# A four-layer graph network on one core: TensorE's turns and ScalarE's copies of them put at other places of the second and third layer, and the load of x first in SyncE's queue in the third

## Chip, cores and metric

One core of one Trainium2 chip runs the whole program. The time is the device time of one execution in microseconds (us). Engines are named as in the profile: PE is TensorE (PEld its weight loads), DVE is VectorE, ACT is ScalarE, POOL is GpSimd, SP is SyncE, which here only issues DMA transfers.

## What is computed

There are 50000 nodes with 128 features (x) and 12500 edges (src, dst), sorted by dst. Four layers follow one another, each of the form x = layernorm(x + layer(x)):

- layer 0: attention over the edges of a node, four heads, softmax by segment;
- layer 1 (the *second* layer): the mean of the neighbours' rows, then relu(([h, mean] @ W1 + b1) @ W2 + b2);
- layer 2 (the *third* layer): the sum over the edges of h[src] @ Wr[relation], eight relations;
- layer 3: messages by edge type, then one of three weight sets by node type, on [relu(h), sums].

```python
x = _layernorm(x + _L1_gnn_ref(x, src, dst, W1, b1, W2, b2))
x = _layernorm(x + _L2_gnn_ref(x, weight, src, dst, edge_type_8))
```

Only nodes that are the dst of some edge (targets) get anything from the sums. All other nodes go through the four layers on their own (the *dense* path), so nodes and edges are worked on at the same time.

## The kernel before

**Tiles.** A block or chunk is C = 500 rows, kept as R = 125 partitions by T = 4 rows. There are NC = 100 dense blocks of nodes and EC = 25 chunks of edges in each layer. For products a tile is *turned* (transposed by TensorE in four pieces into PSUM, `turn`, L1130) and copied by ScalarE into SBUF with features on 128 partitions.

**The dense path.** Block d passes three steps that lie LAG = 3 blocks apart: load and bias (xin, y0), normalize to x1, turn and copy to xt, product with wab (z); then y1, normalize to x3, turn and copy with relu to rt, the type products (three weight sets at once, into po beside z) and the selection sel, normalize to res, store to out. In one dense step the kernel therefore turns x3 of block d-LAG (`turn_rt`, L1175) and x1 of block d (`turn_xt`, L1182). Both use the PSUM bank pt, so the second turn waits until ScalarE has copied the first. `dense_products` (L1195) waits until DVE has read po of the step before (s_read), writes the bias, adds the type products (L1148) and z (L1207) and raises s_z, on which DVE's `read` waits.

**The second layer** (`for c in range(EC)`, L1319 on PE, L818 on DVE, L1054 on ACT, L327 on SP, L522 on POOL) handles edge chunk c with dense block 52 + c. The source rows xs come by a load by SP (L304) and then, where a source is itself a target, four indirect gathers by POOL over it (L434). The target rows xd, same and aux come by three loads of SP (`targets1`, L306) on the semaphore aux. xs has three buffers, xd, same and aux two. `rows1(c+2)` and `targets1(c+1)` wait for s_ln of chunk c-1, that is until DVE has written the scales nmr (L671) of that chunk, after which its rows are not read any more. PE turns xs and xd through one bank pc, one after the other (`turns1`, L1293), and ACT copies them to st and dt (L973, L978). `products1` (L1302) forms the products of both; the product with agg (L1322) ends the chunk. DVE scans st into run and agg (`source_sums1`, L791), adds, measures and writes the scales.

An iteration of ACT: copy rt and xt of the dense step, copy st and dt of chunk c+1, the roots of chunk c (Ln, Exp on the variances, L921), wait for s_ln, then six groups of four normalizing activations (L918): x3, x1, so, so3, do, res. SP stores so and so3 when nS is raised (behind so3), do when nD is, res when s_out is (L314 to L336). SP's queue is in order: load of x, load of xs, three loads of targets1, stores of so, so3, do, res.

**The third layer** (L1351 on PE, L852 on DVE, L1077 on ACT, L372 on SP, L546 on POOL) handles chunk c with dense block 79 + c. DVE multiplies st with (rel == r) into masked for eight relations (L838), the first EARLY = 2 of them one iteration ahead, between the variances and the scales; PE adds the eight products up in pb (`relations2`, L1337, 16 matmul records a chunk); DVE scans pb into run; PE turns that back to rows in pa (L1356). Its iteration before: pa, turn of x3, turn of x1, all relations of c+1, turn of xs of c+2 (`turns2`, L1331), dense products. ACT's: copy rt and xt, copy st of chunk c+2, roots, x3, x1, do, res. SP's: `sources2(c+3)` (waits until xs of chunk c+1 has been turned), load of x, rel, xd and same, stores of do and res. POOL's: four gathers of xs, bias on x (L449, waits for xin), four gathers of node types.

Of the kernel before, what the change touches and what calls it, by code (L numbers as in the profile page):

```python
# [13 lines left out]
D = 128  # L14
R = 125
T = 4
# [29 lines left out]
def gnn_kernel(nc, x, src, dst, srcP, dstP, nextP, eattrT, etype3, etype8, eweight, ntype3, ntypeP, Wq, Wk, Wv, We, gate,  # L46
# [26 lines left out]
    with ctx:  # L73
# [122 lines left out]
        def _(sp):  # L196
# [175 lines left out]
            for c in range(EC):  # L372
                d = block_of(2, c)
                if there(c + 3):
                    sources2(c + 3)
                if d + 2 < NC:
                    load_dense(d + 2)
                if there(c + 2):
                    relations2(c + 2)
                if there(c + 1):  # L380
                    targets2(c + 1)
                if c >= 1:
                    store2(c - 1)
                store_dense(d - 7)
# [526 lines left out]
        def _(act):  # L911
# [16 lines left out]

            def rows_of(d, s, groups):

                first, second = groups
                if 0 <= d - LAG < NC:
                    normalize(x3[(d - LAG) % 4], y1[(d - LAG) % 4], s, second).then_inc(s_x3, 1)
                if 0 <= d < NC:
                    normalize(x1[d % 4], y0[d % 4], s, first).then_inc(s_x1, 1)
# [191 lines left out]
        def _(pe):  # L1127
# [66 lines left out]

            def dense_products(d):  # L1195

                first, second = (0 <= d - k < NC for k in (0, LAG))
                if first or second:
                    pe.wait_ge(s_read, d + 3)
                    biased_slots(NT + 1)  # L1200
                if second:
                    pe.wait_ge(s_rt, d - 2)
                    last = types(lambda j: rt[:, j, :], 0)
                if first:
                    pe.wait_ge(s_xt, d + 1)
                    for j in range(T):
                        last = mm(po[0:R, j * 512 + NT * D:(j + 1) * 512], xt[:, j, :], wab[:, 0, :], start=False, stop=True, skip_group_check=True)  # L1207
                if first or second:
                    last.then_inc(s_z, 1)
# [83 lines left out]
            def turns1(c):  # L1293
                b, q = c % 2, ph[1]
                pe.wait_ge(q["g"][b], counted(c, 16 * T))
                pe.wait_ge(q["aux"][b], counted(c, 48))
                pe.wait_ge(q["eD"], c)
                turn(pc, xs[c % 3]).then_inc(q["tS"], 1)
                pe.wait_ge(q["eS"], c + 1)
                turn(pc, xd[b]).then_inc(q["tD"], 1)  # L1300

            def products1(c):  # L1302
# [4 lines left out]
                product(pa, lambda j: tile_of(st, j), wab[:, 0, :])  # L1307
                pe.wait_ge(q["eD"], c + 1)
# [8 lines left out]
            turns1(0)  # L1317
            products1(0)
            for c in range(EC):  # L1319
# [17 lines left out]
            def relations2(c):  # L1337
                q = ph[2]
                pe.wait_ge(q["vA"], c)
                for r in range(REL):  # L1340
# [8 lines left out]
            relations2(0)  # L1349
            turns2(1)  # L1350
            for c in range(EC):  # L1351
# [88 lines left out]
```

## Time and profile before

| | us |
|---|---|
| runs, median (lowest to highest) | 2155.61 (2153.47 to 2155.76) |
| profiled execution, its own time | 2157.94 |
| its span, first to last instruction | 2155.8 |
| PE busy | 1613.2 (75%) |
| DVE busy | 1479.8 (69%) |
| POOL busy | 1385.2 (64%) |
| ACT busy | 1087.1 (50%) |
| mean granted TensorE clock | 0.85 |

The span is the time between the first and the last instruction of the profiled execution; the execution's own time is 2.1 us more. Busy shares are means over four layers of different kinds. In the windows the granted clock is 1.00 at 2.4 GHz and 0.50 at 1.2 GHz, and the DMA share is the mean busy share of the core's 16 DMA engines. A word such as "issue" in the chain is time in which an engine waited for nothing that the profile can name.

### The profile page before, as it was taken

How to read it: one execution, taken by the hardware profiler on the slowest of the kernel's cores; microseconds unless marked ns; L12 is line 12 of the kernel's file. 1: busy time of each engine (PE TensorE's matmuls, PEld its weight loads, DVE VectorE, ACT ScalarE, POOL GpSimd, SP SyncE). 2: the span in 40 equal slices, each digit the busy share in tenths (PEclk: the TensorE clock that was granted, in tenths of full speed). 3: DMA queues.
4: the chain of work that ended last, by engine and by line, in shares of the span. 5: the costliest groups of instructions: out<-in, count | busy, mean ns of one | idle time of the engine just before them, and what ended most of it. 6: DMA issues, size and time to landing. Idle time of an engine off the chain costs nothing.

```text
span 2155.8 us, 23908 instructions
## 1 busy us (share of the span) xinstructions
PE 1613.2 (75%) x6303; PEld 993.3 (46%) x6303; DVE 1479.8 (69%) x4219; ACT 1087.1 (50%) x2688; POOL 1385.2 (64%) x1060
## 2 busy tenths in 40 slices
PE   3777777777776377776776677777778499999995
PEld 1444444444444255555554344444444145555553
DVE  4788999988889377677776667776677444444453
ACT  0466666666666466777667243444343323233322
POOL 6888877788884667776660656555664146656663
PEclk7688888888888687888778788888889699999998
DMA  4333333333331344444443333333232122222221
GB/s 122 83 84 91 92 90 92 94 91 90 95 91 53 94 120 142 148 141 141 140 139 98 100 93 89 99 99 95 86 94 73 53 58 72 63 60 64 71 60 27
DMA packets 150726, 198.86 MB, mean 92 GB/s; under 512 B 54874, under 2 KB 82844, under 8 KB 150592
## 3 DMA queue, kind: packets, MB, share of 16 engines
q1 hardware_dynamic: 92992, 173.20, 25.7%
q0 software_dynamic: 57600, 24.15, 6.6%
q8 instruction: 51, 0.84, 0.2%
q14 instruction: 83, 0.68, 0.1%
HBM read 140.85 MB, written 70.88 MB: 98 GB/s over the span
## 4 chain that ended last, share of the span: by engine, by line
PE 58%; ACT 17%; issue 12%; DVE 7%; POOL 3%; DMA 2%; SPq 1%; POOLq 0%; ACTq 0%; DVEq 0%
PE po L1148 19%; PE pb L1342 10%; PE pt L1133 7%; ACT x L918 6%; PE po L1143 4%; ACT res L918 3%; PE pc L1133 3%; ACT st L973 3%; PE po L1207 2%; PE pb L1154 2%; DVE masked L838 2%; ACT do L918 1%; PE pc L1238 1%; ACT so L918 1%; PE pb L1379 1%
## 5 line engine op out<-in xcount | busy, mean ns | idle before, releaser
L434 POOL DMA_INDIRECT xs<-target_rows,slot_all x300 | 405.7, 1352 | 246.7 <-DMA xs<-source_rows 97.1
L918 ACT ACTIVATE x<-y,nmr,rst 125x128 f32<-125x128 f32 x800 | 318.5, 481 | 80.1 <-DVE nmr L671 80.0
L1148 PE MATMUL po<-wnt,rt 128*125 128x384 f32 x800 | 310.9, 537 | 0.2 <-ACT rt L948 0.2
L1133 PE MATMUL pt<-ident,x 125*128 125x125 f32 x800 | 144.2, 310 | 199.0 <-issue 182.4
L449 POOL TENSOR_TENSOR y<-xin,bias_bc 125x512 f32<-125x512 f32 x100 | 133.7, 1338 | 205.9 <-DMA xin<-in_x 201.4
L1148 PEld LDWEIGHTS po<-wnt,rt 128*125 128x125 f32 x800 | 174.2, 218 | 117.8 <-issue 40.8
L1342 PE MATMUL pb<-masked,wr 128*128 128x500 f32 x400 | 218.1, 709 | 1.5 <-DVE masked L838 1.5
L441 POOL DMA_INDIRECT out_rows<-do,last_all x100 | 120.2, 1202 | 145.2 <-ACT do L918 107.9
L838 DVE SCALAR_TENSOR_TENSOR masked<-rel,st 128x500 f32<-128x500 int32 x200 | 121.6, 670 | 132.8 <-ACT st L973 132.8
L1133 PEld LDWEIGHTS pt<-ident,x 125*128 125x128 f32 x800 | 105.2, 162 | 232.5 <-issue 207.0
L1143 PE MATMUL po<-ball,ones_bf 128*125 128x512 bf16 (+1 forms) x512 | 163.4, 452 | 51.1 <-DVE sel L688 48.7
L1148 PE MATMUL po<-wnt,run 128*125 128x384 f32 x600 | 197.6, 486 | 0.0
L918 ACT ACTIVATE do<-yd,nmr,rst 125x128 f32<-125x128 f32 x400 | 163.8, 480 | 56.0 <-DVE nmr L671 56.0
L643 DVE BATCH_NORM_STATS2 bst<-y 125x6 f32<-125x128 f32 x800 | 164.8, 279 | 3.6
L973 ACT ACTIVATE st<-pc 128x500 f32<-128x500 f32 x50 | 29.4, 587 | 272.1 <-PE pc L1133 272.1
L717 DVE TENSOR_TENSOR_SCAN run<-same,run,masked 128x500 f32<-128x500 f32 x75 | 89.3, 1243 | 111.6 <-DMA same<-same_d 85.9
L434 POOL DMA_INDIRECT xs<-in_x,src_all x100 | 130.9, 1309 | 50.3 <-issue 27.8
L918 ACT ACTIVATE res<-sel,nmr,rst 125x128 f32<-125x128 f32 x400 | 161.4, 480 | 1.7 <-DVE nmr L671 1.7
L441 POOL DMA_INDIRECT slot_d<-eid,last_all x100 | 137.8, 1378 | 27.8 <-issue 27.1
L434 POOL DMA_INDIRECT xd<-in_x,dst_all x100 | 130.1, 1301 | 30.5 <-issue 30.2
L434 POOL DMA_INDIRECT slot_all<-slot_d,src_all x100 | 128.4, 1284 | 30.4 <-issue 30.4
L434 POOL DMA_INDIRECT ntd_all<-in_ntype,dst_all x100 | 128.7, 1287 | 28.2 <-issue 27.9
(182 smaller groups left out, 3211.0 us busy)
## 6 DMA issues: line engine op xcount, KB each, us to landing
xin<-in_x SPq DMA_DIRECT2D x100, 250.0 KB
out_rows<-res SPq DMA_DIRECT2D x100, 250.0 KB
source_rows<-so SPq DMA_DIRECT2D x75, 250.0 KB
target_rows<-do SPq DMA_DIRECT2D x75, 250.0 KB
xs<-source_rows SPq DMA_DIRECT2D x75, 250.0 KB
xd<-target_rows SPq DMA_DIRECT2D x75, 250.0 KB
same<-same_d SPq DMA_DIRECT2D x75, 250.0 KB
aux<-start_d SPq DMA_DIRECT2D x25, 250.0 KB
```

The costliest lines, as they stand in the source:

```text
L434: return nc.gpsimd.indirect_dma_start(out=to, out_offset=None, in_=table, in_offset=bass.IndirectOffsetOnAxis(ap=index, axis=0), bounds_ch ...
L441: return nc.gpsimd.indirect_dma_start(out=table, out_offset=bass.IndirectOffsetOnAxis(ap=index, axis=0), in_=of, in_offset=None, bounds_ch ...
L449: nc.gpsimd.tensor_tensor(y0[d % 4][:, :, :], xin[d % 4][:, :, :], bias_rows, ALU.add).then_inc(s_y0, 1)
L643: last = V.bn_stats(bst[s][:, g * T + j, :], y[:, j, :])
L717: return V.tensor_tensor_scan(m[:, k, 1:C + 1], data0, data1, m[:, k, 0:1] if start is None else start, op0, op1)
L838: V.scalar_tensor_tensor(out=masked[:, r, :], in0=rel[b][:, :], scalar=float(r), in1=st[:, :], op0=ALU.is_equal, op1=ALU.mult).then_inc(q[ ...
L918: last = A(to[:, j, :], y[:, j, :], ACT.Identity, scale=rst[s][:, k:k + 1], bias=nmr[s][:, k:k + 1])
L973: A(st[:, :], bank[k][:, 0:C], ACT.Copy).then_inc(q["eS"], 1)
L1133: last = nc.tensor.transpose(tile_of(to, j), rows_[:, j, :], ident[0:R, 0:R])
L1143: mm(po[0:R, j * 512:j * 512 + n * D], ones_bf[:, 0:R], ball[:, 0:n, :].rearrange("k s d -> k (s d)"), start=True, stop=False, skip_group_ ...
L1148: last = mm(po[0:R, j * 512:j * 512 + NT * D], left(j), wnt[:, k, :, :].rearrange("k t d -> k (t d)"), start=False, stop=stop, skip_group_ ...
L1342: mm(pb[:, 0:C], wr[:, r, :], masked[:, r, :], start=r == 0, stop=r == REL - 1).then_inc(q["pM"], 1)
```

## The change

SP, third layer: `load_dense(d + 2)` is put ahead of `sources2(c + 3)`.

ACT, second layer: the copies of the next dense step and of chunk c+2 are taken apart and put between the groups: x3, copy rt, copy st(c+2), x1, so, copy xt, copy dt(c+2), so3, do, res. Chunks 0 and 1 are copied ahead of the loop. Third layer: x3, copy rt, x1, copy st(c+3) (once all masks of c+2 are made), copy xt, do, res; chunks 0, 1 and 2 are copied ahead of the loop.

PE, second layer: pb of agg, turn x3, turn xs(c+1), type products, turn x1, turn xd(c+1), product of st, z, product of dt. The turn of xs waits for its gathers only; the semaphore aux is waited for by the turn of xd. Third layer: pa, turn x3, relations 0 to 3 of c+1, turn xs(c+2), turn x1, relations 4 to 7, dense products.

```diff
             for c in range(EC):
                 d = block_of(2, c)
+                if d + 2 < NC:
+                    load_dense(d + 2)
                 if there(c + 3):
                     sources2(c + 3)
-                if d + 2 < NC:
-                    load_dense(d + 2)
...
             evacuate_sources(0, 1, 7)
             evacuate_targets(0, 1, 7, dt, ACT.Copy)
+            evacuate_rt(block_of(1, 0) - 2)
+            evacuate_sources(1, 1, 7)
+            evacuate_xt(block_of(1, 0) - 2)
+            evacuate_targets(1, 1, 7, dt, ACT.Copy)
             for c in range(EC):
                 b, q = c % 2, ph[1]
                 d = block_of(1, c)
                 k = chain_of(d)
-                evacuate_dense(d - 2)
-                if there(c + 1):
-                    evacuate_sources(c + 1, 1, 7)
-                    evacuate_targets(c + 1, 1, 7, dt, ACT.Copy)
                 first_roots(k % 2, 6)
                 act.wait_ge(s_ln, k + 1)
-                rows_of(d, k % 2, (3, 0))
+                third_rows(d, k % 2, 0)
+                if there(c + 1):
+                    evacuate_rt(d - 1)
+                if there(c + 2):
+                    evacuate_sources(c + 2, 1, 7)
+                first_rows(d, k % 2, 3)
                 act.wait_ge(q["stS"][b], (c // 2) * 32)
                 normalize(so[b], ys[b], k % 2, 4)
+                if there(c + 1):
+                    evacuate_xt(d - 1)
+                if there(c + 2):
+                    evacuate_targets(c + 2, 1, 7, dt, ACT.Copy)
                 normalize(so3[b], ys[b], k % 2, 1).then_inc(q["nS"], 1)
...
             evacuate_sources(1, 2, 7)
+            evacuate_rt(block_of(2, 0) - 2)
+            act.wait_ge(ph[2]["vM"], 2 * REL)
+            evacuate_sources(2, 2, 7)
+            evacuate_xt(block_of(2, 0) - 2)
             for c in range(EC):
...
-                evacuate_dense(d - 2)
-                if there(c + 2):
-                    act.wait_ge(q["vM"], (c + 2) * REL)
-                    evacuate_sources(c + 2, 2, 7)
                 first_roots(k % 2, 4)
                 act.wait_ge(s_ln, k + 1)
-                rows_of(d, k % 2, (2, 0))
+                third_rows(d, k % 2, 0)
+                if there(c + 1):
+                    evacuate_rt(d - 1)
+                first_rows(d, k % 2, 2)
+                if there(c + 3):
+                    act.wait_ge(q["vM"], (c + 3) * REL)
+                    evacuate_sources(c + 3, 2, 7)
+                if there(c + 1):
+                    evacuate_xt(d - 1)
                 act.wait_ge(q["stD"][b], (c // 2) * 16)
                 normalize(do[b], yd[b], k % 2, 3).then_inc(q["nD"], 1)
...
                 d = block_of(1, c)
-                dense_turns(d - 2)
-                if there(c + 1):
-                    turns1(c + 1)
-                dense_products(d - 2)
-                if there(c + 1):
-                    products1(c + 1)
+                turn_rt(d - 2)
+                if there(c + 1):
+                    turn_sources1(c + 1)
+                type_products(d - 2)
+                turn_xt(d - 2)
+                if there(c + 1):
+                    turn_targets1(c + 1)
+                    source_products1(c + 1)
+                z_products(d - 2).then_inc(s_z, 1)
+                if there(c + 1):
+                    target_products1(c + 1)
...
                 d = block_of(2, c)
-                dense_turns(d - 2)
-                if there(c + 1):
-                    relations2(c + 1)
+                turn_rt(d - 2)
+                if there(c + 1):
+                    relations2(c + 1, range(REL // 2))
                 if there(c + 2):
                     turns2(c + 2)
+                turn_xt(d - 2)
+                if there(c + 1):
+                    relations2(c + 1, range(REL // 2, REL))
                 dense_products(d - 2)
```

`third_rows` and `first_rows` are the two halves of `rows_of`; `turn_sources1`, `turn_targets1`, `source_products1`, `target_products1`, `type_products` and `z_products` are the pieces of `turns1`, `products1` and `dense_products`, with the same waits:

```python
def turn_sources1(c):
    pe.wait_ge(q["g"][b], counted(c, 16 * T))
    pe.wait_ge(q["eD"], c)
    turn(pc, xs[c % 3]).then_inc(q["tS"], 1)

def turn_targets1(c):
    pe.wait_ge(q["aux"][b], counted(c, 48))
    pe.wait_ge(q["eS"], c + 1)
    turn(pc, xd[b]).then_inc(q["tD"], 1)
```

## Rows read from the trace of the kernel before

**Rows 1.** Windows by layer (second, third); columns: us, busy (instructions), PEclk, DMA share, GB/s
```profile
752.00:1157.00 405.00, 294.36 (x1504) 221.97 (x1503) 291.12 (x962) 283.53 (x714) 265.69 (x201) 0.81 0.44 136
...
1203.00:1680.00 477.00, 375.22 (x1266) 214.80 (x1265) 345.30 (x996) 193.06 (x492) 274.85 (x213) 0.85 0.32 90
```

**Rows 2.** One line's instructions (L1154 agg, L1356): first and last start
```profile
L1154 PE MATMUL pb<-wab,agg x200: 272/273/273, 753.0 to 1157.1; 128*125 128x128 f32 x100
...
L1356 PE MATMUL pa<-ident,run x100: 272/273/375, 1214.8 to 1675.3; 128*125 128x128 f32 x100
```

**Rows 3.** Timeline of SP, second layer: start us, us, line, transfer
```profile
1003.18 0.27 SPq L317 DMA_DIRECT2D source_rows<-so  x1
...
1013.41 0.25 SPq L304 DMA_DIRECT2D xs<-source_rows  x1
...
1014.52 1.17 SPq L312 DMA_DIRECT2D aux<-rdeg_d  x1
```

**Rows 4.** Timeline of all engines, same period
```profile
1022.81 1.27 POOL L434 DMA_INDIRECT xs<-target_rows,slot_all  x1 [2.49 <-DMA xs<-source_rows]
...
1026.09 1.06 PE L1133 MATMUL pc<-ident,xs 125*128 125x125 f32 x4 [2.19 <-issue]
...
1027.83 1.09 PE L1133 MATMUL pc<-ident,xd 125*128 125x125 f32 x4 [0.68 <-ACT st L973]
...
1028.96 0.59 ACT L978 ACTIVATE dt<-pc 128x500 f32<-128x500 f32 x1 [1.19 <-PE pc L1133]
...
1030.82 3.19 ACT L918 ACTIVATE x<-y,nmr,rst 125x128 f32<-125x128 f32 x8 [0.90 <-DVE nmr L671]
```

**Rows 5.** Windows of 1 us: second layer twice, third, fourth; last columns DMA share, GB/s
```profile
1010.00:1011.00 1.00, 0.62 (x3) 0.62 (x4) 0.97 (x4) 0.33 (x1) 0.69 (x2) 0.50 0.34 124
1021.00:1022.00 1.00, 0.09 (x1) 0.00 (x0) 1.00 (x7) 1.00 (x4) 0.00 (x0) 1.00 0.34 114
1401.00:1402.00 1.00, 1.00 (x4) 0.54 (x3) 0.00 (x0) 0.00 (x0) 0.69 (x2) 1.00 0.01 0
1865.00:1866.00 1.00, 1.00 (x4) 0.52 (x3) 0.91 (x1) 0.00 (x0) 1.00 (x1) 1.00 0.35 120
```

**Rows 6.** Timeline of SP and TensorE at the start of the second layer
```profile
768.90 0.27 SPq L317 DMA_DIRECT2D source_rows<-so  x1
...
778.02 0.25 SPq L304 DMA_DIRECT2D xs<-source_rows  x1
...
790.26 1.07 PE L1133 MATMUL pc<-ident,xs 125*128 125x125 f32 x4 [1.75 <-issue]
```

**Rows 7.** Chain that ended last, third layer: start us, us, what
```profile
1383.76 0.84 PE pb L1342 x2
...
1406.41 3.20 ACT x L918 x8
1409.61 3.63 issue
1413.24 1.07 PE pt L1133 x4
1414.31 8.50 PE pb L1342 x16
```

**Rows 8.** Timeline of VectorE over one period of the third layer
```profile
1406.31 1.25 DVE L717 TENSOR_TENSOR_SCAN run<-same,run,pb 128x500 f32<-128x500 f32 x1
...
1418.62 0.16 DVE L658 TENSOR_SCALAR ve<-ve 125x12 f32<-125x12 f32 x1
1423.95 1.27 DVE L838 SCALAR_TENSOR_TENSOR masked<-rel,st 128x500 f32<-128x500 int32 x2 [5.17 <-ACT st L973]
...
1425.87 1.26 DVE L717 TENSOR_TENSOR_SCAN run<-same,run,pb 128x500 f32<-128x500 f32 x1
```

**Rows 9.** Groups by line on GpSimd, third layer: xcount | busy, mean ns | idle before
```profile
L434 POOL DMA_INDIRECT ntd_all<-in_ntype,dst_all x100 | 128.7, 1287 | 28.2 <-issue 27.9 <-DMA xs<-source_rows 0.3
...
L449 POOL TENSOR_TENSOR y<-xin,bias_bc 125x512 f32<-125x512 f32 x19 | 25.3, 1330 | 105.6 <-DMA xin<-in_x 105.6
```

More of the change, by code:

```diff
@@ L927, in first_roots, with third_rows, first_rows, rows_of @@
                 A(seed[s][:, 0:n * T], seed[s][:, 0:n * T], ACT.Exp, scale=-0.5).then_inc(s_seed, 1)
-            def rows_of(d, s, groups):
-                first, second = groups
+            def third_rows(d, s, second):
                 if 0 <= d - LAG < NC:
                     normalize(x3[(d - LAG) % 4], y1[(d - LAG) % 4], s, second).then_inc(s_x3, 1)
+            def first_rows(d, s, first):
                 if 0 <= d < NC:
                     normalize(x1[d % 4], y0[d % 4], s, first).then_inc(s_x1, 1)
+            def rows_of(d, s, groups):
+                third_rows(d, s, groups[1])
+                first_rows(d, s, groups[0])
             def results_of(d, s, third):
@@ L1193, in dense_turns, with type_products, z_products @@
                 turn_xt(d)
+            def type_products(d):
+                pe.wait_ge(s_read, d + 3)
+                biased_slots(NT + 1)
+                pe.wait_ge(s_rt, d - 2)
+                return types(lambda j: rt[:, j, :], 0)
+            def z_products(d):
+                pe.wait_ge(s_xt, d + 1)
+                for j in range(T):
+                    last = mm(po[0:R, j * 512 + NT * D:(j + 1) * 512], xt[:, j, :], wab[:, 0, :], start=False, stop=True, skip_group_check=True)
+                return last
             def dense_products(d):
                 first, second = (0 <= d - k < NC for k in (0, LAG))
-                if first or second:
+                if second:
+                    last = type_products(d)
+                elif first:
                     pe.wait_ge(s_read, d + 3)
                     biased_slots(NT + 1)
-                if second:
-                    pe.wait_ge(s_rt, d - 2)
-                    last = types(lambda j: rt[:, j, :], 0)
                 if first:
-                    pe.wait_ge(s_xt, d + 1)
-                    for j in range(T):
-                        last = mm(po[0:R, j * 512 + NT * D:(j + 1) * 512], xt[:, j, :], wab[:, 0, :], start=False, stop=True, skip_group_check=True)
+                    last = z_products(d)
                 if first or second:
@@ L1291, in _, with source_products1 @@
                     dense_products(2 * c + 1)
-            def turns1(c):
+            def turn_sources1(c):
                 b, q = c % 2, ph[1]
                 pe.wait_ge(q["g"][b], counted(c, 16 * T))
-                pe.wait_ge(q["aux"][b], counted(c, 48))
                 pe.wait_ge(q["eD"], c)
                 turn(pc, xs[c % 3]).then_inc(q["tS"], 1)
+            def turn_targets1(c):
+                b, q = c % 2, ph[1]
+                pe.wait_ge(q["aux"][b], counted(c, 48))
                 pe.wait_ge(q["eS"], c + 1)
                 turn(pc, xd[b]).then_inc(q["tD"], 1)
-            def products1(c):
+            def source_products1(c):
                 q = ph[1]
@@ L1307, in products1, with target_products1 @@
                 product(pa, lambda j: tile_of(st, j), wab[:, 0, :])
+            def target_products1(c):
+                q = ph[1]
+                pe.wait_ge(q["rd"], c)
                 pe.wait_ge(q["eD"], c + 1)
@@ L1316, in _ @@
             pe.wait_ge(ph[0]["nF"], EC)
-            turns1(0)
-            products1(0)
+            turn_sources1(0)
+            turn_targets1(0)
+            source_products1(0)
+            target_products1(0)
             for c in range(EC):
@@ L1335, in turns2, with relations2 @@
                 turn(pc, xs[b]).then_inc(q["tS"], 1)
-            def relations2(c):
+            def relations2(c, relations):
                 q = ph[2]
                 pe.wait_ge(q["vA"], c)
-                for r in range(REL):
+                for r in relations:
                     pe.wait_ge(q["vM"], c * REL + (r + 1))
@@ L1348, in _ @@
             turns2(0)
-            relations2(0)
+            relations2(0, range(REL))
             turns2(1)
```

## Prediction

> **What bounds the kernel now.** I read four views in this order: the windows by layer, the transfers that SyncE (SP) issues, the DMA share microsecond by microsecond, and the chain that ended last. The first says where the change can act: the second layer takes 405 us, the third 477 us, and in neither is an engine busy all the time [rows 1]. A period (one chunk of 500 edges plus one dense block) is (1157.1 - 753.0)/24 = 16.84 us in the second layer and (1675.3 - 1214.8)/24 = 19.19 us in the third [rows 2]. The two layers are bound by different things.
>
> In the **second layer** TensorE looks as if it were held by its own order: it stands idle for 2.19 us ahead of the turn of xs. What it waits for there is the semaphore aux, set by three loads (xd, same, aux) that SP issues only when VectorE has written nmr. SP issued its four loads from 1013.41 to 1015.7 [rows 3]. GpSimd saw xs land at 1022.81, and TensorE got past aux at 1026.09; the gathers of that chunk had been issued a period before, so it was aux [rows 4]. The landing is thus 12.7 us behind the issue, for 250 KB copies. The windows say why: the DMA share stands at 0.34 and 114 to 124 GB/s in each microsecond of the period outside the bursts of the broadcasts, which is about five of sixteen engines, never idle. A single copy of 125 rows running by itself in the last layer shows the same 0.35 and 120 GB/s, and in the third layer the share does fall to 0.01 [rows 5]. So a 250 KB copy of 125 rows costs 256/118 = 2.2 us on engines that all such copies share, seven of them (so, so3, do, res, xin, xs, xd) make 15.2 us, and two broadcasts and the gathers fill up the 16.84. The second layer is bound by this queue, and it is full only because the stores of one chunk (so at 1003.18 [rows 3]) are issued while loads of a later one are still on their way.
>
> The Trainium skill (DMA: Bandwidth & Descriptors, the section on why a DMA increments its semaphore by 16) says that a copy is spread over the largest number of engines up to 16 that divides its slowest dimension; for 125 rows that would be 5. By that rule the trace agrees: 0.34 of 16 is 5.4.
>
> In the **third layer** the chain goes round once a period: the normalizing groups x3, x1, do and res on ScalarE (3.20 and 3.63), the turn of x1 (1.07), sixteen passes of the relation products (8.50), the turn of xs, its copy, two masks and the scales, and back [rows 7]. ScalarE sits behind the relation products with the roots queued after them. Here order is the bound.
>
> **The second layer, part by part.** (a) TensorE takes the turn of xs out from behind aux and places type products between its turns. It has 12 to 13 us of work in a period and doesn't bound the layer, so I cost this at nothing; its cover is the queue. (b) ScalarE copies rt and st behind x3, and xt and dt between so and so3, in iteration c and for chunk c+2. That is the costly edit. SP issues targets1(c+2) only after s_ln of chunk c; before, the copy of dt(c+2) stood at the head of the next iteration, behind all groups of c. Now so3, do and res of chunk c wait for a load that the same iteration's nmr has just released. Behind the waiting instruction on ScalarE stand so3, do, res and the next roots; behind so3 stands nS, and behind nS SP with both stores of so and everything after them. So the five copies so to xin, 11 of the 16.84 us, can't start until the loads have landed, and the queue runs empty in each period.
>
> The new period, from one landing of aux to the next: the turn of xd and its wait until dt is copied and so3 can start, 1028.96 - 1027.83 + 0.5 = 1.6 us; so3 itself, half of 3.19; the issue by SP: 3.3 us together [rows 4]. Then the whole round of copies, 16.84 us. Between them lie the start of the first copy and the notice of the last. No row has it alone, so I bound it: at the layer's start the queue was nearly empty, and from the issue of so at 768.90 to aux at 790.26 went 21.4 us, the loads having been issued at 778.02 [rows 6]; that is 4.5 over 16.84, and a rest of the earlier batch is in it. So it is 0 to 4.5 us, and I take the middle, 2.3, since both latency and that rest must be in the 4.5. Period: 3.3 + 16.84 + 2.3 = 22.4 us, bounds 20.1 and 24.7. It holds for chunks with a chunk c+2; the first has no stores ahead of it (I take 17.7) and the last doesn't wait (15): 17.7 + 22 x 22.4 + 15 = 526 against 404, **+121 us**, bounds +71 and +172.
>
> ScalarE needs 1.6 us, three groups at 1.54 and 1.4 for roots and scales (1030.82 - 1028.96 less the 0.5 of the copy) [rows 4], 7.6 us, from that landing to the next nmr, well within 22.4, so it adds nothing.
>
> **The third layer, part by part.** (c) Half of the relation products now come ahead of the turn of xs for chunk c+3, half behind the turn of x1; ScalarE copies st(c+3) one iteration earlier, when masks(c+2) are done. That takes the relation products out of the chain: roots wait only for VectorE's variances and for res. What is late next is VectorE: from its scan to the end of the variances (1418.78 - 1406.31 = 12.47 us), then masks and scales (1425.87 - 1423.95 = 1.92 us), **14.4 us** with no gap [rows 8]. ScalarE: the turn of x1 comes behind vA (1.3 us after nmr), the transposes, the turn of x3, four relations (3.4) and the turn of xs, so xt is copied by about 7.1, and do and res end 3.2 later, some 10.3 us after nmr, under 12.5. TensorE: 375/25 = 15.0 us busy in a period at a mean clock of 0.85 [rows 1]; with the clock up the sixteen passes take 6.7 us at 0.42 in place of 8.5 and the turn of x1 half of 1.07 [rows 7], which leaves 12.7 us. Its longest idle stretch would be under 2 us against more than 3.6 now, so I expect the granted clock near 1. GpSimd: eight indirect DMAs at 1.29 + 0.28 and the bias 1.33 + 0.2, 14.1 us [rows 9]. Copies: five at 2.2 and the rest 1.6, 12.6 us. Four resources lie within 2 us of each other, so I take 14.6 us for the period, bounds 14.4 and 15.6. (d) The load of x goes first in SP's queue. Now GpSimd waits 105.6 us in all for xin [rows 9], since SP's x load is queued behind one that waits for the turn of xs. It moves past the loads of xs and rel, which each come 0.3 us later; their cover is several microseconds until the gathers need them. Without this edit GpSimd, at 14.1 us of work, would soon set the period, so it belongs to (c). Sum: 24 x (19.19 - 14.6) = **-110 us**, bounds -86 and -115.
>
> **Sum.** +121 - 110 = +11 us on the span of 2155.8, or 2166.8; that execution took 2157.9, 2.1 more, and the median of the runs shown is 2155.6, so 2167 us in terms of the median. The number is a small difference of two large terms, and its sign hangs on the second layer.
>
> **Rivals.**
> The queue absorbs the wait (faster). If 12.7 us is a backlog that shrinks when less is queued, aux could land so early that the copy of dt costs nothing. Its point of decision: the landing would have to come 16.84 - 7.6 = 9.2 us after nmr. Against it: res and xin are issued within 3 us ahead of the loads, five copies at 2.2 us can't drain by then, and the share of 0.34 was never below saturation. For it: the first periods of the layer. Then -110 alone, with up to +20: 2046 to 2066. Chance 0.13.
>
> The bubble is small (faster). The period is 19.6 to 20.1, because gathers use the empty stretch and the copies pack closer: +60 to +71, in sum -50 to -39, 2106 to 2117. It needs seven copies in about 13 us where rows show 15.2. Chance 0.10. The same page of the Trainium skill gives some 27 GiB/s for an engine (Specifications), by which five engines would need an estimated 1.8 us for a copy and the period would be near 19.6; the trace has 2.2, which I use.
>
> The third layer gains half (slower). Copies, GpSimd and VectorE, each over 85% busy, take turns in waiting, or TensorE's clock stays down: a period of 17, -53, in sum +68, 2224. Chance 0.12.
>
> The forecast itself, +121 and -110 within their bounds, has 0.65; its own range is 2140 to 2205.
>
> **How the numbers follow.** A measurement of this kernel tells about 0.2%, 4.3 us, from no change. Of the forecast's 0.65, 0.09 falls below -4.3, 0.08 within and 0.48 above. Faster: 0.13 + 0.10 + 0.09 = 0.32; same 0.08; slower 0.48 + 0.12 = 0.60. The range from 2090 to 2215 leaves out the first rival and about half of the third.
>
> **What would show it.** Second layer: ScalarE's copy of dt stands between so and so3 with an idle stretch of several microseconds before it, ended by TensorE's turn of xd, which itself waited; starts of the agg product lie 22 us apart; the DMA share falls to nearly nothing in each period. Third layer: VectorE without idle stretches, starts of the pa transposes 14.6 us apart, granted clock near 1, GpSimd's wait for xin mostly gone. If the second layer keeps 17 us or its DMA share stays at 0.34 throughout, step (b) is wrong; if the third keeps idle stretches on VectorE, (c) is.

## The result, and the profile after

The changed kernel takes 2239.6 us (2235.8 to 2240.2, four runs) against 2155.7 in the same session: 1.0383 times before, 95% interval 1.0364 to 1.0403. The profiled execution has a span of 2238.1 us and an own time of 2240.2. Windows by layer of the changed kernel (us, PE, PEld, DVE, ACT, POOL, PEclk, DMA share, GB/s), to be held against [rows 1]:

```profile
753.00:1294.00 541.00, 302.05 (x1505) 239.57 (x1504) 280.05 (x954) 276.17 (x695) 262.78 (x200) 0.80 0.36 100
1361.00:1759.00 398.00, 335.78 (x1238) 195.72 (x1239) 335.42 (x973) 191.14 (x482) 273.72 (x205) 0.92 0.39 106
```

First and last start of the two lines of [rows 2], changed kernel:

```profile
L1178 PE MATMUL pb<-wab,agg x200: 272/273/418, 754.8 to 1293.9; 128*125 128x128 f32 x100
L1405 PE MATMUL pa<-ident,run x100: 272/273/573, 1361.3 to 1758.8; 128*125 128x128 f32 x100
```

The second layer's period is (1293.9 - 754.8)/24 = 22.46 us for 16.84, the third's (1758.8 - 1361.3)/24 = 16.56 for 19.19. The stretch between the two lines was 1214.8 - 1157.1 = 57.7 us and is 67.4. So +135.0 in the second layer, -63.0 in the third and +9.7 between make +81.7, nearly all of the 82.3 by which the span grew (2238.1 - 2155.8).

The chain of waits of the changed kernel over one period of the second layer (start us, us, what):

```profile
903.06 10.87 DMA aux<-rdeg_d
...
913.97 1.11 PE pc L1157 x4
...
915.10 0.59 ACT dt L985
915.69 1.53 ACT so L918 x4
917.22 1.54 ACT do L918 x4
918.76 1.55 ACT res L918 x4
...
920.33 0.65 SPq L227
...
921.03 1.33 SPq L222
...
925.99 10.85 DMA aux<-rdeg_d
...
936.89 1.11 PE pc L1157 x4
```

It is the loop that was forecast: landing of aux, turn of xd, copy of dt, so3 (its line reads "so"), then the stores and loads, landing again. The two parts of the forecast's sum can be read off. From the landing (903.06 + 10.87 = 913.93) to the end of so3 at 917.22 are 3.3 us, as forecast; from there to the next landing at 936.84 are 19.6 us, for 16.84 + 2.3. The chain itself fills those 19.6 us with do, res, five issues by SP one behind the other (920.33 to 925.99, 5.7 us) and aux's landing 10.85 us behind its issue. The timeline shows how ScalarE stands still meanwhile (dt's copy, behind an idle stretch of 9.00 us), and a window of 1 us how the queue runs dry, where the second layer's windows in [rows 5] have a share of 0.34:

```profile
936.89 1.09 PE L1157 MATMUL pc<-ident,xd 125*128 125x125 f32 x4 [8.49 <-DMA aux<-rdeg_d]
...
938.02 0.59 ACT L985 ACTIVATE dt<-pc 128x500 f32<-128x500 f32 x1 [9.00 <-PE pc L1157]
```

```profile
914.00:915.00 1.00, 1.00 (x5) 1.00 (x6) 0.99 (x1) 0.00 (x0) 0.69 (x2) 0.50 0.00 0
```

In the third layer periods of 14 and 20 us take turns: VectorE writes nmr at 1528.1, 1542.5 and 1562.7. The timeline of the changed kernel, with what leads to the longer one:

```profile
1525.80 0.40 SPq L222 DMA_DIRECT2D xin<-in_x  x1
...
1535.65 1.27 POOL L449 TENSOR_TENSOR y<-xin,bias_bc 125x512 f32<-125x512 f32 x1 [5.36 <-DMA xin<-in_x]
...
1548.82 1.27 POOL L434 DMA_INDIRECT xs<-target_rows,slot_all  x1 [0.30 <-issue]
...
1554.88 1.09 PE L1157 MATMUL pc<-ident,xs 125*128 125x125 f32 x4 [5.93 <-DMA xs<-target_rows,slot_all]
...
1556.07 0.59 ACT L980 ACTIVATE st<-pc 128x500 f32<-128x500 f32 x1 [8.31 <-PE pc L1157]
...
1560.89 1.29 DVE L838 SCALAR_TENSOR_TENSOR masked<-rel,st 128x500 f32<-128x500 int32 x2 [5.81 <-PE pb L1391]
```

VectorE does idle (5.81 us ahead of the masks), because TensorE waited 5.93 us for the gathers of xs ahead of the turn of xs, with half of the relation products behind it. The last of these gathers starts at 1548.82. They stand in GpSimd's queue behind the bias on x and four gathers of node types, and the bias could start only at 1535.65, 9.8 us behind the issue of the load of x (1525.80). The loop closes over ScalarE: xt, do and res stand behind the copy of st, which idled for 8.31 us ahead of it, and SP issues the load of x behind the store of res. Two periods on, at 1560.85, it issues it again, 35 us later.

Over the whole layer ScalarE idles 110.1 us ahead of this copy, the largest of its waits there (xcount | busy, mean ns | idle before):

```profile
L980 ACT ACTIVATE st<-pc 128x500 f32<-128x500 f32 x23 | 13.5, 587 | 110.1 <-PE pc L1157 83.5 <-issue 26.6
```

### The profile page after: what moved, and what is told of

It reads as the page before. It is cut to its first block, busy times and chain, and to the rows that moved or that the text cites. A ratio compares the mean times of both kernels' runs of the same rounds, so it can differ in the third digit from the quotient of the medians.

```text
span 2238.1 us, 23982 instructions
## 1 busy us (share of the span) xinstructions
PE 1596.8 (71%) x6303; PEld 999.2 (45%) x6303; DVE 1467.6 (66%) x4219; ACT 1089.7 (49%) x2688; POOL 1387.4 (62%) x1060
## 4 chain that ended last, share of the span: by engine, by line
PE 29%; ACT 18%; DMA 15%; issue 14%; POOL 10%; DVE 7%; SPq 7%; POOLq 0%; ACTq 0%; DVEq 0%
PE po L1172 12%; DMA aux<-rdeg_d 11%; POOL xs L434 5%; ACT res L918 4%; PE pt L1157 4%; ACT do L918 3%; ACT x L918 3%; ACT so L918 3%; POOL ntd_all L434 2%; PE po L1167 2%; SPq L310 1%; PE pc L1273 1%; SPq L222 1%; DVE run L717 1%; PE pc L1157 1%
## 5 line engine op out<-in xcount | busy, mean ns | idle before, releaser
L434 POOL DMA_INDIRECT xs<-target_rows,slot_all x300 | 410.6, 1369 | 357.2 <-DMA xs<-source_rows 218.5
L918 ACT ACTIVATE x<-y,nmr,rst 125x128 f32<-125x128 f32 x800 | 323.2, 483 | 78.9 <-DVE nmr L671 71.5
L1167 PE MATMUL po<-ball,ones_bf 128*125 128x512 bf16 (+1 forms) x512 | 154.7, 432 | 57.8 <-DVE sel L688 50.2
L1391 PE MATMUL pb<-masked,wr 128*128 128x500 f32 x400 | 194.8, 635 | 1.5 <-DVE masked L838 1.5
L1157 PE MATMUL pt<-ident,x 125*128 125x125 f32 x800 | 135.8, 297 | 44.3 <-issue 28.7
L1157 PE MATMUL pc<-ident,xd 125*128 125x125 f32 x100 | 26.2, 413 | 179.5 <-DMA aux<-rdeg_d 178.7
L1172 PEld LDWEIGHTS po<-wnt,run 128*125 128x125 f32 x600 | 110.7, 188 | 74.5
```

The lines of the kernel that those rows point to most:

```text
L434: return nc.gpsimd.indirect_dma_start(out=to, out_offset=None, in_=table, in_offset=bass.IndirectOffsetOnAxis(ap=index, axis=0), bounds_ch ...
L918: last = A(to[:, j, :], y[:, j, :], ACT.Identity, scale=rst[s][:, k:k + 1], bias=nmr[s][:, k:k + 1])
L1157: last = nc.tensor.transpose(tile_of(to, j), rows_[:, j, :], ident[0:R, 0:R])
L1167: mm(po[0:R, j * 512:j * 512 + n * D], ones_bf[:, 0:R], ball[:, 0:n, :].rearrange("k s d -> k (s d)"), start=True, stop=False, skip_group_ ...
L1172: last = mm(po[0:R, j * 512:j * 512 + NT * D], left(j), wnt[:, k, :, :].rearrange("k t d -> k (t d)"), start=False, stop=stop, skip_group_ ...
L1391: mm(pb[:, 0:C], wr[:, r, :], masked[:, r, :], start=r == 0, stop=r == REL - 1).then_inc(q["pM"], 1)
```

## Experiments

Each is the changed kernel with one edit, unless said otherwise. The two columns of periods (us) are worked out as above, from first and last start of the same two lines in the one profiled execution. Each ratio is to the kernel before as timed beside that run, whose medians lay between 2153.6 and 2158.8.

| | second | third | median us | ratio to before, 95% interval |
|---|---|---|---|---|
| before | 16.84 | 19.19 | 2155.7 | |
| changed | 22.46 | 16.56 | 2239.6 | 1.038 [1.036, 1.040] |
| e1 second layer of before | 16.72 | 16.65 | 2099.9 | 0.975 [0.971, 0.979] |
| e2 third layer of before | 22.55 | 19.23 | 2301.4 | 1.068 [1.065, 1.071] |
| e3 dt behind res | 19.23 | 16.58 | 2161.2 | 1.004 [1.001, 1.006] |
| e11 st and dt behind res | 19.93 | 16.70 | 2178.9 | 1.011 [1.008, 1.014] |
| e14 TensorE's old order, second | 22.80 | 16.78 | 2242.1 | 1.039 [1.033, 1.044] |
| e13 ScalarE's old order, second | 20.14 | 16.39 | 2187.4 | 1.013 [1.010, 1.016] |
| e4 e1 and x one block ahead | 16.93 | 15.62 | 2068.2 | 0.959 [0.957, 0.962] |
| e15 x behind xs again, third | 22.53 | 17.23 | 2261.5 | 1.050 [1.046, 1.054] |
| e9 e3 and x one block ahead | 19.71 | 15.60 | 2136.6 | 0.989 [0.985, 0.993] |
| e5 before, copies cut | 16.96 | 19.21 | 2158.2 | 1.001 [0.999, 1.004] |
| e6 changed, copies cut | 15.45 | 15.45 | 2045.9 | 0.947 [0.942, 0.951] |
| e10 e4, copies cut | 16.56 | 14.58 | 2046.4 | 0.949 [0.946, 0.952] |
| e12 x ahead, copies cut | 15.54 | 14.59 | 2029.5 | 0.940 [0.937, 0.943] |
| e7 e12 and dt behind res | 14.50 | 14.54 | 1998.6 | 0.925 [0.921, 0.928] |

### Which layer: e1 and e2

e1 takes back the second layer on PE and ACT, e2 the third on PE, ACT and SP.

> The changed kernel with TensorE's and ScalarE's order of the second layer as before; the third layer's change stays. Theory: the two layers' effects add up, +135 us in the second layer (24 periods of 22.46 against 16.84), -63 in the third (16.56 against 19.19) and +10 on the way from the second to the third, which belongs to the second. Then this run takes 2155.7 - 63 = 2093 us, with agg starts 16.8 us apart and pa starts 16.6 apart. Rival: the 10 us on the way belong to the third layer's new copies ahead of its loop: 2103. Rival of the forecast: the third layer was slowed by what the second left in the queues, and by itself comes to 14.6 us a period: about 2046.

> The changed kernel with the third layer as before on all engines, SP's order too; the second layer's change stays. Theory: +135 in the second layer and +10 on the way to the third: 2300 us, agg starts 22.5 us apart. If the 10 us belong to the third layer's change: 2291.

The two changes add up: the spans are 2093.9 (-61.9) and 2298.5 (+142.7), together +80.8 for the +82.3 of both. The stretch between the layers is 58.6 us in e1 and 66.7 in e2, so its 9 us belong to the second layer's change.

### Where in the second layer: e3, e11, e14, e13

e3:

```diff
-                if there(c + 2):
-                    evacuate_targets(c + 2, 1, 7, dt, ACT.Copy)
                 normalize(so3[b], ys[b], k % 2, 1).then_inc(q["nS"], 1)
...
                 results_of(d, k % 2, 2)
+                if there(c + 2):
+                    evacuate_targets(c + 2, 1, 7, dt, ACT.Copy)
```

> The changed kernel, but ScalarE copies dt of chunk c+2 behind res instead of between so and so3. Everything else of the change stays, TensorE's order too. Theory: the place of this one copy is the whole loss of the second layer; stores go out while loads are under way, the DMA share no longer falls to zero, the period is that of the full queue, 16.8 us: some 2093 to 2103 us in all. Rival: the other moves (turns set apart by products, st and xt copied between the groups) hold the layer up by themselves: the period stays above 19 us and the time above 2155. Rival: the period falls below 16.8, to 15.5 or so, since the queue was never the bound: 2065.

Not the theory but the first rival came, a period above 19 us. The period falls by 3.2 us, 78 us of the layer's 135; 2.4 us a period stay. The landing of aux no longer closes its chain; the loop goes over the source rows, and so3, do and res lie on it behind the copy of xt instead of dt's:

```profile
952.65 12.43 DMA xs<-source_rows
...
971.12 8.68 DMA xs<-target_rows,slot_all
...
979.85 0.65 PE pc L1157 x4
980.49 1.55 PE po L1167 x4
...
986.09 0.59 ACT xt L961
986.68 1.53 ACT so L918 x4
...
989.75 1.54 ACT res L918 x4
...
993.07 12.00 DMA xs<-source_rows
```

A load that lands after 12.43 us, four gathers on GpSimd, the last of which lands after 8.68, the turn of xs, and behind it the type products and the turn of x1, which the new order puts there; then xt's copy, so3, do, res and, after the scales, the next load but one: 40.4 us for two periods. Is it the early copy of st that holds x1 up? e11 moves that copy behind res too:

> e3_dt_behind_res, and ScalarE's copy of st of chunk c+2 also goes behind res. TensorE's order stays as changed. In e3 the second layer's period was 19.2 us, in turns 21 and 17, and the longer ones wait for the gathers of xs: nmr of chunk c, load of xs(c+3), gathers, turn of xs two iterations later, copy of st between x3 and x1, and behind it all other groups of ScalarE. Theory: this copy is the rest of the loss, and without it the period is 16.8 to 17.3 us, 2100 to 2115 us in all. Rival: TensorE's turn of xs ahead of the type products holds z and so VectorE, wherever ScalarE copies st: the period stays at 19 us or so, 2160.

```diff
                 third_rows(d, k % 2, 0)
-                if there(c + 2):
-                    evacuate_sources(c + 2, 1, 7)
                 first_rows(d, k % 2, 3)
...
                 results_of(d, k % 2, 2)
                 if there(c + 2):
+                    evacuate_sources(c + 2, 1, 7)
                     evacuate_targets(c + 2, 1, 7, dt, ACT.Copy)
```

19.93 us: no gain, a loss (ratio 1.011 for 1.004, the intervals apart). The place of st's copy is not it. No run moves the copy of xt, or gives TensorE its old order, with dt's copy behind res, so which edit holds the 2.4 us stays open; the rows name the type products and xt's copy behind them.

e14 gives TensorE the order of before in the second layer, e13 gives ScalarE its own (the lines of the change taken back):

```diff
-                turn_rt(d - 2)
+                dense_turns(d - 2)
                 if there(c + 1):
                     turn_sources1(c + 1)
-                type_products(d - 2)
-                turn_xt(d - 2)
-                if there(c + 1):
                     turn_targets1(c + 1)
+                dense_products(d - 2)
+                if there(c + 1):
                     source_products1(c + 1)
-                z_products(d - 2).then_inc(s_z, 1)
-                if there(c + 1):
                     target_products1(c + 1)
```

> The changed kernel with TensorE's order of before in the second layer (both turns of x, then both turns of the chunk, then all products), ScalarE's order and everything else as changed. The forecast's step (a), that this order costs and gives nothing: the period stays at 22.5 us and the time at 2240 (2230 to 2250). Rival, that the new order of TensorE is what keeps ScalarE's late wait from costing more: the turn of xd then waits for its load with the type products and z queued behind it, some 5 us of products come between the landing and VectorE's next variances, and the period grows by 3 to 5 us: 2310 to 2360. Third, that the products between the turns are what the other 2.4 us of the period are (those that stayed when only dt's copy was moved): the period falls to about 20, 2180.

> The changed kernel with ScalarE's order of before in the second layer, TensorE's order and everything else as changed. ScalarE then copies rt, xt, st and dt one behind the other at the head of an iteration, while TensorE turns x1 only behind the type products, which need rt: three to four us of products come into the chain, less the 2.2 us that TensorE waited for the loads there. Period 18.5 to 20.5 in the second layer for 22.5: 2130 to 2180. Rival, that TensorE's order is free with any order of ScalarE (step (a)): as with the whole second layer of before, 2095 to 2105.

With ScalarE's new order TensorE's is worth 0.3 us a period and nothing in the median (2242.1 for 2239.6): the landing of aux closes the loop either way. With ScalarE's old order TensorE's new one costs 20.14 - 16.72 = 3.4 us (e13 against e1). The chain of e13 has this piece in it:

```profile
916.93 1.54 ACT res L918 x4
918.47 0.48 ACT rt L955
...
918.99 4.62 PE po L1163 x8
923.61 0.44 PE pt L1148 x4
924.07 0.59 ACT xt L961
```

ScalarE's copy of xt, with st, dt and the roots behind it, now waits for 4.62 us of type products. Up to 1.5 of the 3.4 us may be another thing, slowed instructions of VectorE, of which e13 has 22 in this layer and e1 one (see the last section).

### The third layer: e4, e15, e9

e4 is e1 with the load of x one block further ahead; e15 is the changed kernel with `load_dense(d + 2)` behind `sources2(c + 3)` again; e9 is e3 with the edit of e4.

```diff
+            load_dense(block_of(2, 0) + 2)
             for c in range(EC):
                 d = block_of(2, c)
-                if d + 2 < NC:
-                    load_dense(d + 2)
+                if d + 3 < NC:
+                    load_dense(d + 3)
```

> As e1_second_old, and SP loads x of block d + 3 in the third layer where it loaded d + 2, so that xin has landed a period before GpSimd asks for it. Theory: the third layer's period of 16.6 us is the loop res, load of x issued, xin landed (10.4 us), bias, four gathers of types, four gathers of xs, their landing, turn of xs two chunks later; with xin out of it VectorE is the bound at 14.4 to 15 us: 40 to 50 us less than e1_second_old, some 2048 us, GpSimd's wait for xin gone. Rival: the shared copy queue or the gathers' own landing is the bound, and the period stays within 0.5 us of e1_second_old's.

> The changed kernel with the load of x back behind the loads of xs in SP's queue, in the third layer only. If the third layer's 16.6 us come from the loop over the x load (res stored, x loaded, bias added, gathers behind it on GpSimd, turn of xs), the load now also waits for the turn that frees the buffer of xs, and the period grows by 0.5 to 2 us: 2252 to 2288. Rival, that the load of x is late by the length of the queue alone and its place among its neighbours is 0.3 us of issue: no change, 2235 to 2247.

> The changed kernel with dt's copy behind res in the second layer and the load of x issued one block further ahead in the third, copies not cut. If the two are independent, the second layer has the 19.2 us of the run with dt behind res and the third the 15.6 of the run with x ahead: 2161 less 24 x 0.95 = 2138 (2130 to 2146). Rival, that the third layer's gain came only beside the second layer of before: 2155 to 2165.

The bias on x over the third layer, groups on GpSimd (xcount | busy, mean ns | idle before), changed kernel and e4; before has it in [rows 9]:

```profile
L449 POOL TENSOR_TENSOR y<-xin,bias_bc 125x512 f32<-125x512 f32 x18 | 22.7, 1260 | 59.6 <-DMA xin<-in_x 59.5
```

```profile
L450 POOL TENSOR_TENSOR y<-xin,bias_bc 125x512 f32<-125x512 f32 x18 | 22.9, 1274 | 0.6
```

The wait is gone and 1 us of the period with it, half of what e4's theory asked for (2068.2 for 2048). e15 costs 0.67 us a period: that is what the first place in the queue is worth, and issuing x a block earlier is worth 1.0 us more. e9 has the one gain in full (15.60) and most of the other (19.71 for 19.23); its profiled execution took 2153.3 us, 17 above its own median, so the 19.71 is rather too high. No run moves st's copy behind res in this layer, as e3 does with dt's in the other; ahead of it ScalarE still idles 58.5 us in e4.

### The length of the copies: e5, e6, e10, e12, e7

The forecast read a share of about five DMA engines for copies of 125 rows. These kernels cut each such copy of SP into 112 and 13 rows (the waits count twice as much); e5 does that to the kernel before, e6 to the changed one.

```diff
+            def move(to, of):
+                for part in (slice(0, 112), slice(112, R)):
+                    yield sp.dma_start(to[part, :], of[part, :])
```

> The kernel before, with each copy of 125 rows that SP issues in the four layers (loads of x, xs, xd; stores of so, so3, do, res) issued as two copies, of 112 and of 13 rows, the semaphore counts doubled. Bytes and order stay. Theory: 125 rows go over five DMA engines of sixteen, and that is what fills the second layer; 112 rows go over sixteen. The DMA share then stands above 0.34 while a copy runs and falls near 0 between, and the second layer's period falls from 16.84 to the loop of its engines, 14.5 to 15.5 us; the third layer, bound by order, keeps 19.2. Some 2110 to 2130 us. Rival: 118 GB/s is a limit of the queue or of the memory, not of five engines: the share and the period stay, and twice the issues on SP cost up to 10 us.

> The changed kernel with the same split of all SP copies of 125 rows. Theory: in the second layer the change puts the landing of aux into the loop of ScalarE (landing + 1.1 + so3, do, res, roots, scales, in all landing + 7.6 us). With five engines the landing took 14 us or more behind nmr, with sixteen it takes 6 to 8, so the period falls from 22.5 to about 14.5 us, below the 16.8 of the kernel before, and the loss turns into a gain; the third layer's loop over xin shortens from 16.6 to about 15. Some 2239.6 - 24 x 8 - 24 x 1.5 = 2010 us. Rival: latency, not rate, makes the landing: the period stays above 19 us and the time above 2150.

> e4_second_old_x_ahead (second layer's order as before, third as changed, x one block ahead) with the same split. Theory: the second layer's period goes from 16.8 to about 15, the third keeps 15.6 or gains 0.5, since VectorE is its bound: 2015 to 2030 us. If it is slower than e6_split_after, the change's order of the second layer is the better one once the copies are quick; if faster, the order before is better with either kind of copy.

e5 didn't come out as expected (2158.2 for 2110 to 2130), and it is the run that says most. Its windows of 1 us show what the cut does: gaps, and bursts at two and a half times the share of [rows 5] (in the 7 us before the second window SP has issued only stores of so, do and res).

```profile
908.00:909.00 1.00, 1.00 (x9) 0.87 (x8) 0.96 (x3) 0.07 (x1) 1.00 (x1) 1.00 0.13 2
...
921.00:922.00 1.00, 0.65 (x3) 0.68 (x4) 0.42 (x2) 0.25 (x1) 0.69 (x2) 0.50 0.89 276
```

The queue of the second layer isn't full any more, and the period is 16.96 for 16.84. Its chain over two periods of the second layer has no transfer in it:

```profile
911.43 3.20 ACT x L937 x8
914.63 6.72 issue
921.35 1.07 PE pt L1152 x4
922.41 0.85 PE pc L1152 x4
...
925.02 1.71 PE po L1162 x4
926.73 3.80 PE po L1167 x8
930.53 0.89 PE po L1226 x8
931.44 0.69 DVE y L701
```

The 6.72 us of "issue" are so, so3, do and res on ScalarE and behind them its copy of rt, which frees the bank for TensorE's turn of x1 at 921.35. Then come the turns, all type products, z, VectorE's variances and scales, and x for the second time, at 945.58: two periods in 34.15 us, 17.1 each. So the order of before holds the layer at about 17 us with no transfer on the chain. A part of it came with the cut: slowed instructions of VectorE, 2.17 us on this chain and some 0.8 us a period over the layer (last section), which would leave 16.2 if all of it lay on the chain. That the copies alone would give 17 as well is the forecast's estimate; no run shows it. The change takes the order away; e6 (15.45) shows what it is worth once the copies are short, and e10, with the order of before, stays at 16.56, up to 0.65 of it by the same slowed instructions. Both are slower than was expected of them (2010 and 2015 to 2030).

> The changed kernel with every copy of 125 rows cut into 112 and 13 rows, and the load of x in the third layer issued one block further ahead. With short copies the second layer should keep the 15.4 us of the run with cut copies alone, and the third fall from 15.4 to the 14.6 of the run that had both: 24 x 0.85 = 20 us less than 2046, so 2025 (2018 to 2032). Rival, that the third layer's 15.4 are not the loads of x but the company of the changed second layer's order or VectorE's slowed instructions: 2040 to 2050.

> As the run with cut copies and x ahead, with ScalarE's copy of dt for chunk c+2 moved behind res as well. If the place of that copy costs only because its load lands late, it costs nothing once the copies are short: within 5 us of that run (2020 to 2030). Rival, that the copy still lies on the chain that now goes round by ScalarE's groups, VectorE and the type products: moving it behind res takes 0.5 us out of each period, 12 us less (2010 to 2016). Second rival, that the wait is still there in part: 20 to 40 us less.

e12 adds x ahead to e6 and has the third layer at 14.59. Windows of e7, second and third layer:

```profile
760.00:1090.00 330.00, 252.01 (x1417) 208.43 (x1418) 267.30 (x907) 257.06 (x651) 262.28 (x199) 0.88 0.61 160
1190.00:1500.00 310.00, 277.24 (x1107) 164.01 (x1106) 302.02 (x863) 175.91 (x442) 259.47 (x189) 1.00 0.45 123
```

e7 is the fastest, 7.5% under before: 14.5 us in both layers. dt's copy behind res takes another 1.04 us a period off, 31 us in the median. That is the size of the second rival (20 to 40 us), not of the main expectation, but the rival's reason isn't it: ahead of dt's copy ScalarE idles only 0.4 us in all in e12's second layer. The cause isn't settled. What the traces show is that ScalarE's wait for the turn of x1 ahead of xt falls from 60.2 us in the layer to 10.9, while its idle time ahead of rt grows from 4.0 to 32.3, and that the granted clock is 0.88 for 0.83 of e12 over the same stretch; which of these is the cause of the others was not tried.

## Why the prediction was right and wrong

The side was right, and the size was not: 2239.6 for 2167, above the range's 2215. The step that failed is (c), the third layer. By its steps:

- **The bound of the second layer** was half read. In the second layer's windows of [rows 5] the queue is not idle, but it wasn't the bound by itself: with the queue relieved (e5) the order of before holds about 17 us. Rows of before that the prediction left out say so (its timeline, same period as [rows 4]):

```profile
1021.08 1.63 ACT L918 ACTIVATE res<-sel,nmr,rst 125x128 f32<-125x128 f32 x4
...
1022.62 0.56 ACT L948 ACTIVATE rt<-pt 128x500 f32<-128x500 f32 x1
...
1023.28 0.62 PE L1133 MATMUL pt<-ident,x 125*128 125x125 f32 x4 [2.20 <-issue]
```

  TensorE's turn of x1 waits for a copy that stands behind all groups of ScalarE. The reading took the wait for aux, the last to end, and didn't ask what period the loop has with that wait at zero.
- **(a)**, TensorE's order costs nothing: right here (e14), because the loop over the landing of aux covers it. It isn't so under ScalarE's old order (3.4 us a period, e13).
- **(b)**, period 22.4: measured 22.46. The mechanism is in the chain, the dry queue in the windows. That it fits to 0.1 us is luck in part, since 2.3 was the middle of 0 to 4.5 and the 16.84 was not the queue's alone. Moving dt's copy alone gives back 3.2 of the 5.6 us (e3); behind it lies the next loop, over the loads and gathers of xs and the type products behind their turn, which the step didn't see. And +121 should have been +145: the first and last chunks weren't cheaper (539 us for 526), and the stretch behind the layer grew by 9.7, which was no term of the sum.
- **(c)**, period 14.6: the step that failed, 16.56 measured and -63 us for -110, 47 of the 73 us by which the time was missed. VectorE's 14.4 us was sized rightly (e10 and e12 reach 14.58 and 14.59, and in e7 VectorE is busy 302 of 310 us). What failed is the overlap. The step took four resources within 2 us of each other to run side by side, and ScalarE's copy of st, now ahead of xt, do and res, to cost nothing: do and res were to end some 10.3 us after nmr. In the longer period they end 17.8 us after it (1542.7 to 1560.5), since the copy waits for the turn of xs. The loop behind that wait wasn't looked for: res stored, x loaded (about 10 us to land), bias, gathers behind it on GpSimd, their landing, the turn of xs, st, do, res. x ahead takes 1.0 us of the 2.0 out (e4). With short copies the other 1.0 goes (e10), but e4 has 1.0 us a period of VectorE's slowed instructions, and e10 next to none, so whose gain that is isn't told apart. The clock was 0.92, not near 1; it is 1.00 in e7.
- **(d)** was right in sign: GpSimd's wait for x fell from 105.6 to 59.5 us, and undoing it costs 16 us over the layer (e15). "Mostly gone" it was not: x comes first in the queue, but SP issues it only behind the store of res.
- **The rivals.** The third, a period of 17 in the third layer because copies, GpSimd and VectorE wait in turn, is what came by its number (16.56), at a chance of 0.12, and its reason names the waiting but not the loop; its 2224 lacks the 24 us of the second layer's ends and has 10 too many in the third. Its chance was too small: four resources within 2 us of each other were taken as a reason for 0.4 us on top, where each also waited for the others' latencies. The two faster rivals didn't come; the first (copies out of the way, the change a gain) is e6, where it takes cut copies, not a shrinking backlog.

## What to carry to other kernels

Before an order of copies is changed, work out the period with each candidate bound set to zero; where two lie close together, as here the queue (by estimate) and the order at about 17 us, removing one shows nothing. An instruction placed earlier on an in-order engine is free only if what it waits for lands before its turn comes, and the landing time to use is that of the loaded queue (10 to 12 us here), not the 2.2 us that the copy itself was reckoned at. Here it paid to make the transfers short first and reorder then: the same change is 3.8% slower on long copies and, with copies cut, 5.2% faster than the cut kernel before (2045.9 to 2158.2).

## Not expected of the hardware

Cut copies (112 and 13 rows) ran far above the 0.34 and 114 to 124 GB/s of copies of 125 rows [rows 5]. A window of 1 us of e6, second layer, with only stores of so, so3, do and res on their way from SP:

```profile
903.00:904.00 1.00, 0.00 (x0) 0.00 (x0) 0.00 (x0) 0.97 (x5) 0.70 (x2) 1.00 0.92 274
```

By the rule of the Trainium skill that the prediction cites (DMA: Bandwidth & Descriptors, the section on why a DMA increments its semaphore by 16), 112 rows, a multiple of 16, would go over all 16 engines; the trace agrees, with a share of 0.92. It isn't free: SP issues twice as many transfers, and e5's second layer starts at 765.5 us for 753.0 (in the kernels with cut copies between 758.0 and 770.3, in the others between 745.6 and 756.1). Where the first layer loses this was not looked into.

Some of VectorE's smallest instructions took 2.2 us instead of 0.17 to 0.2. Timeline of e4, third layer, two places:

```profile
1402.33 2.26 DVE L655 TENSOR_TENSOR ve<-ve,tmp 125x16 f32<-125x16 f32 x1
1403.28 1.28 POOL L450 TENSOR_TENSOR y<-xin,bias_bc 125x512 f32<-125x512 f32 x1
```

```profile
1420.80 2.17 DVE L671 SCALAR_TENSOR_TENSOR rst<-tmp,seed 125x16 f32<-125x16 f32 x1
1421.65 1.26 POOL L450 TENSOR_TENSOR y<-xin,bias_bc 125x512 f32<-125x512 f32 x1
```

In both places GpSimd's bias on x runs, and VectorE's instruction, with two inputs, ends when it ends. The Trainium skill (SBUF — State Buffer, SBUF: two separate sides) says that a VectorE instruction with two SBUF inputs and a GpSimd instruction that reads SBUF exclude each other for a whole instruction. The two places agree; that VectorE's instruction takes 0.9 us longer than GpSimd's recorded 1.26 isn't explained by it, nor is a TENSOR_SCALAR of VectorE with one input that took 2.29 us in the same way (e4, at 1320.56).

It bears on the runs above. Counting VectorE's instructions of 4 to 24 elements that took over 1 us, and what they took over 0.18 us each, the second layer has 22 in e13 (36 us, 1.5 a period), 11 in e5 (19 us, 0.8 a period), 9 in e10 (16 us, 0.65 a period), one each in the kernel before and in e1, and none in the changed kernel, e6, e7 and e12. The third has 13 in e4 (25 us, 1.0 a period) and in e9 (26 us), 7 in e6, and at most one in the kernel before, the changed kernel, e7, e10 and e12. In e13, e4, e5, e10, e9 and e6 every one of them ends within 0.15 us of a bias on GpSimd. So an edit that moves the bias against VectorE's scales changes the period by up to 1.5 us that its own theory doesn't hold. No run moved the bias off, so what it costs in the period, as against in these instructions, is open.
